# Self-attention on one core: compact reciprocals by DMA, even score slots, weighted values two key chunks at a time, and three short chains of probability tiles

## The chip, the core and the metric

The kernel runs on one core of a Trainium2 chip. Five engines work side by side and meet only through semaphores: TensorE (PE in the profile, its weight loads PEld), VectorE (DVE), ScalarE (ACT), GpSimd (POOL) and SyncE (SP, which here only issues DMAs). The metric is the device time of one execution in microseconds. Before the change it is 3310.52 us, the median of three runs (3309.83 to 3311.77).

## The reference

A decoder layer over x of shape (2, 2048, 512): layer norm and self-attention, cross-attention to 154 context rows, and a feed-forward part with a shared and eight chosen experts. The change touches the self-attention alone. Cut to it:

```python
B, S, D = (2, 2048, 512); H = 16; HEAD_DIM = 32; BLOCK = 512
qkv = (layernorm(x) @ w_qkv.T)                     # q, k, v: (b, H, s, 32)
for k_blk, v_blk in blocks_of(k, v, BLOCK):        # a softmax that is built up block by block
    scores = einsum('bhid,bhjd->bhij', q, k_blk) / sqrt(32)
    ...
    out = ... + exp(block_max - new_lse) * einsum('bhij,bhjd->bhid', exp(scores - block_max), v_blk)
x = x + out @ w_out.T
```

That equals softmax(q k^T / sqrt(32)) v for each head. The kernel works it out in two passes: the row maxima first, then the exponentials, their sums and the weighted values.

## The kernel before, in words

`self_attention` runs over 32 **units**. A unit is one batch, four heads (a quad) and a block of 512 queries; four units in a row share a quad's keys and values. A unit has 16 **steps** `k`, one for each chunk of 128 keys. In step `k` PE does, in this order (`body` of the tensor block):

- for each of the four heads, the transposed scores of the **next** chunk (`transposed_scores`, L698, into `ps_st`, three banks), and between them some **score slots** of the **next unit** (`scores`, L679, into `ps_s`, three banks). A slot is 128 queries by 512 keys of one head, and only its row maximum is wanted. A unit has 64 slots; `SLOTS_AT` says how many stand in each step, and 8 early ones stand in steps 14 and 15 of the unit before that.
- in steps 7 and 14 (`TURN_AT`) four small matmuls (`turn_max`, L690) that turn half of the next unit's row maxima into a row, which ACT copies into `q_stack` (L861, L862). Before step 15 PE waits until ACT has copied the second half, because the next unit's transposed scores start there.
- the weighted values of chunk `k` (`weighted_values`, L709, four heads side by side in four column strips, accumulated in `ps_pv`), a group of four fp32 matmuls that the trace shows as eight. After step 8 and step 14 a group of the same shape follows that sums a tile of probabilities over the keys with `ones` (L717, `TOTALS_AT`), and after step 3 one for the unit before (`added_totals`, L724). These sums are the softmax denominators, in `ps_d`.

ACT takes each transposed score tile from its bank with an exponential (L880) into `probs`, a ring of 8 chunks, and at a unit's end copies `ps_pv` to `attn_raw` (L886). DVE takes each score slot with a maximum (L778, `slot_max`); a bank of `ps_s` is free for PE again only when its maximum is done (`max_done`). POOL adds up ten of the 16 probability chunks in `added` (`add`, L637); the other six are added in two chains of three by DMAs that accumulate in SBUF (`link`, L645, issued by POOL).

When the denominators of a unit are complete, DVE inverts `ps_d` in four pieces of 128x128 between score slots (`invert`, L803), multiplies with `attn_raw` (`normalize`, L810), and SP stores the result (L583). SP also loads queries four units ahead (L565) and, at the end of each quad, the keys and values of the quad after the next (L572, L577), on the same queue as the store.

## Time and profile before

| what | value |
|---|---|
| median of three runs | 3310.52 us |
| the profiled execution | 3310.81 us, span of its instructions 3309.0 us, mean clock 0.940 |
| self-attention in it | first score matmul at 344.2 us, last normalization at 2149.0 us |
| busy over the span | PE 3018.6 us (91%), DVE 2198.7 (66%), POOL 1725.8 (52%), ACT 1623.4 (49%) |
| DVE reciprocals of the denominators | 128 of 128x128, 121.0 us in all |
| accumulating DMAs | 128 of 1024 KB, median 7.0 us from issue to landing |

The profile's times are those of one execution and count from its first instruction. "Busy" for PE is modelled from pipelined matmuls, so 91% says that PE is nearly always holding work, not that it computes at its peak; how fast it goes is read from the starts of neighbouring matmuls. A bracket at a row's end gives the engine's idle time just before it and what ended it.

### The profile page before, as it was taken

The numbers are of one execution on the slowest core, as the hardware profiler recorded it, in microseconds if no ns is written. First come the engines' busy times: TensorE is split into PE (matmuls) and PEld (weight loads), VectorE is DVE, ScalarE is ACT, GpSimd is POOL, SyncE is SP. The second block draws the span as 40 slices with busy tenths as digits, with TensorE's granted clock in tenths as the row PEclk, the third lists the DMA queues.
The fourth block names the chain that finished last, engine by engine and source line by source line (L and its number), as shares of the span: only waits on it lengthen the run. The fifth ranks groups of instructions, "written<-read, shape, count | busy, mean of one in ns | idle before, by whom it ended". The sixth has DMA issues, their size and how long they took to land. (4 is left out here: it accounts for less than half of the span.)

```text
span 3309.0 us, 41856 instructions
## 1 busy us (share of the span) xinstructions
PE 3018.6 (91%) x15214; PEld 1726.3 (52%) x15214; DVE 2198.7 (66%) x3919; ACT 1623.4 (49%) x2965; POOL 1725.8 (52%) x697
## 2 busy tenths in 40 slices
PE   8998799999999999999999999789579995889488
PEld 5787344444444444444444444268454553777433
DVE  4331888888888888888888888255348694666323
ACT  2222166666666666666666667522136572222111
POOL 0000288888787878787878788800112001333255
PEclk9999599999999999999999999889878797999689
DMA  7444744744646446446374444269655243333621
GB/s 232 179 167 154 178 102 87 156 91 104 143 104 142 102 99 144 105 106 137 87 156 86 106 120 98 62 196 251 153 141 155 79 120 112 127 142 113 210 79 36
DMA packets 171933, 426.85 MB, mean 129 GB/s; under 512 B 19393, under 2 KB 40802, under 8 KB 151716
## 3 DMA queue, kind: packets, MB, share of 16 engines
q1 hardware_dynamic: 147614, 279.59, 28.9%
q0 software_dynamic: 24128, 144.75, 20.8%
q8 instruction: 115, 1.88, 0.2%
q14 instruction: 76, 0.62, 0.1%
HBM read 172.29 MB, written 126.67 MB: 90 GB/s over the span
## 5 line engine op out<-in xcount | busy, mean ns | idle before, releaser
L778 DVE TENSOR_REDUCE part_max<-ps_s 128x1 f32<-128x512 f32 x2048 | 1270.9, 680 | 305.4 <-PE ps_s L679 305.4
L880 ACT ACTIVATE probs<-ps_st 128x512 f32<-128x512 f32 x2048 | 1086.2, 600 | 548.3 <-PE ps_st L698 526.6
L637 POOL TENSOR_TENSOR added<-added,probs 128x2048 f32<-128x2048 f32 x256 | 1185.6, 4631 | 90.4 <-ACT probs L880 63.5
L679 PE MATMUL ps_s<-k_stack,q_stack 96*128 96x512 f32 x2048 | 841.4, 427 | 28.1 <-POOL max_parts L627 20.7
L698 PE MATMUL ps_st<-q_stack,k_stack 98*128 98x512 f32 x2048 | 861.2, 426 | 5.2 <-ACT probs L880 3.9
L698 PEld LDWEIGHTS ps_st<-q_stack,k_stack 98*128 98x128 f32 x2048 | 388.3, 190 | 508.9 <-ACT probs L880 358.8
L709 PE MATMUL ps_pv<-probs,v_sb 128*32 128x512 f32 x4096 | 549.3, 608 | 0.0
L679 PEld LDWEIGHTS ps_s<-k_stack,q_stack 96*128 96x128 f32 x2048 | 395.0, 193 | 214.5 <-DVE part_max L778 143.8
L645 POOL DMA_DIRECT2D probs<-probs x128 | 111.5, 871 | 230.3 <-PE ps_pv L709 219.2
L1366 PE MATMUL xps_s<-xks_stack,xq_stack 99*128 99x154 f32 (+1 forms) x512 | 122.8, 319 | 55.7 <-DVE xident_r L1479 48.8
L637 POOL TENSOR_TENSOR added<-probs 128x2048 f32<-128x2048 f32 x32 | 146.4, 4575 | 47.2 <-ACT probs L880 47.2
L709 PEld LDWEIGHTS ps_pv<-probs,v_sb 128*32 128x32 f32 x4096 | 80.9, 108 | 152.0 <-ACT probs L880 123.7
L1447 DVE TENSOR_REDUCE xneg_max<-xps_s 128x2 f32<-128x308 f32 x256 | 114.8, 476 | 68.1 <-PE xps_s L1369 45.9
L803 DVE RECIPROCAL ps_d<-ps_d 128x128 f32<-128x128 f32 x128 | 121.0, 950 | 57.6 <-PE ps_d L724 57.6
L1366 PEld LDWEIGHTS xps_s<-xks_stack,xq_stack 99*128 99x128 f32 (+1 forms) x512 | 114.2, 224 | 73.3 <-issue 54.0
L286 DVE TENSOR_TENSOR qk_l_out<-ps_g,qk_h_out 128x512 fp32r<-128x512 f32 x64 | 43.3, 689 | 124.9 <-ACT qk_h_out L350 124.9
L238 POOL TENSOR_TENSOR rstd<-var_eps,minus_half 128x4 f32<-128x4 f32 x8 | 8.1, 1014 | 224.2 <-DVE var_eps L264 224.2
L1393 PE MATMUL xps_st<-xq_stack,xkt_stack 98*77 98x512 f32 x256 | 118.6, 468 | 4.4 <-ACT xprobs L1511 2.4
L1511 ACT ACTIVATE xprobs<-xps_st,xpad_bias 77x512 f32<-77x512 f32 x192 | 119.1, 677 | 4.4 <-PE xps_st L1393 3.8
L1465 DVE RECIPROCAL xsums<-xsums 128x256 f32<-128x256 f32 x64 | 111.1, 1742 | 6.1 <-ACT xsums L1524 6.1
L1702 POOL MEMSET e_bias_rows<- 128x1024 f32 x1 | 1.0, 957 | 209.0 <-POOLq L46 209.0
L350 ACT ACTIVATE qk_h_out<-ps_g 128x512 fp32r<-128x512 f32 x64 | 38.3, 598 | 144.4 <-PE ps_g L398 144.4
(266 smaller groups left out, 3567.0 us busy)
## 6 DMA issues: line engine op xcount, KB each, us to landing
probs<-probs POOLq DMA_DIRECT2D x128, 1024.0 KB, 7.0
xq_stack<-q_parts SPq DMA_DIRECT2D x64, 384.0 KB, 4.5
q_stack<-q_hi SPq DMA_DIRECT2D x64, 256.0 KB, 6.3
k_stack<-k_hi SPq DMA_DIRECT2D x64, 256.0 KB, 8.7
q_parts<-q_h_out SPq DMA_DIRECT2D x64, 256.0 KB, 4.9
x_in<-in_x_rows SPq DMA_DIRECT2D x8, 1024.0 KB, 7.0
q_hi<-qk_h_out SPq DMA_DIRECT2D x8, 1024.0 KB, 4.3
q_lo<-qk_l_out SPq DMA_DIRECT2D x8, 1024.0 KB, 6.3
```

The lines of the kernel that those rows point to most:

```text
L637: pool.tensor_tensor(added[:, w % 2], left, probs[:, k % RING], ALU.add).then_inc(added_up, 1)
L645: pool.dma_start(probs[:, k % RING].rearrange("p j q -> p (j q)"), probs[:, (k - 1) % RING].rearrange("p j q -> p (j q)"), accum_op=ALU.ad ...
L679: pe.matmul(ps_s[:, place % BANKS], q_stack[0:ROWS, w % 4, j, t * P:(t + 1) * P], k_stack[0:ROWS, w // BPB, j, n * BLK:(n + 1) * BLK], sta ...
L698: pe.matmul(ps_st[:, n % BANKS], k_stack[0:TOP, w // BPB, j, k * P:(k + 1) * P], q_stack[:, w % 4, j], start=True, stop=True).then_inc(ite ...
L709: mm = pe.matmul(ps_pv[j * HD:(j + 1) * HD], v_sb[:, w // BPB, k, j * HD:(j + 1) * HD], probs[:, k % RING, j], start=(k == 0), stop=(k == ...
L778: dve.tensor_reduce(part_max[:, s:s + 1], ps_s[:, (w * SLOTS + s) % BANKS], AX.X, ALU.max)\
L803: dve.reciprocal(ps_d[:, cols], ps_d[:, cols]).then_inc(inverted, 1)
L880: act.activation(probs[:, k % RING, j], ps_st[:, n % BANKS], ACT.Exp, scale=SCALE).then_inc(item_used, 1)
L1366: mm = pe.matmul(out, q_stack[0:top, u % BUFS, j, t * P:(t + 1) * P], ks_stack[0:top, batch(u), u % QUADS * HEADS + j], start=True, stop=n ...
L1393: mm = pe.matmul(out, kt_stack[:, batch(u), u % QUADS * HEADS + j, h * KH:(h + 1) * KH], q_stack[0:TOP, u % BUFS, j], start=True, stop=not ...
L1447: dve.tensor_reduce(neg_max[:, u % 2, s // 2, s % 2 * 2:s % 2 * 2 + 2], ps_s[:, (u * SLOTS + s) % BANKS, 0:2 * SC].rearrange("p (t k) -> p ...
L1511: act.activation(probs[:, u % 2, t % 2, t // 2], ps_st[0:KH, n % BANKS], ACT.Exp, scale=SCALE, **bias)\
```

## The change

Five edits, all in the self-attention:

1. PE does nothing of the weighted values in even steps; in each odd step it does those of chunks `k-1` and `k` one after the other.
2. `SLOTS_AT` becomes four slots in each of steps 0 to 13 (before: 4, 4, 4, 4, 3, 3, 2, 4, 5, 5, 5, 5, 4, 4), so that with the early ones each of the 16 steps has four.
3. The two chains of three chunks become three chains of two (2+3, 6+7, 8+9), each one accumulating DMA. Their sums come after steps 9, 13 and 15, which makes three groups with `ones` in place of two. POOL issues three such DMAs per unit in place of four, and its nine adds take chunks 0, 1, 4, 5 and 10 to 15.
4. The denominators no longer are inverted in `ps_d` by DVE. ACT copies them to SBUF in step 4 (`dens_out`); SP moves one row per head to DRAM and back as 128x16; DVE inverts that in one instruction before the first slot of step 7; SP moves it to DRAM, and four DMAs read it back with each row repeated over 32 partitions into `attn_out`.
5. POOL multiplies `attn_out` with `attn_raw` (`product`) after its fifth add. The last unit alone is inverted and multiplied by DVE as before, in one piece of 128x512.

```diff
-    SLOTS_AT = [4, 4, 4, 4, 3, 3, 2, 4, 5, 5, 5, 5, 4, 4, 0, 0]
+    SLOTS_AT = [4] * 14 + [0, 0]
-    ADDED = [0, 4, 5, 9, 10, 11, 12, 13, 14, 15]
-    CHAINS = [(1, 2, 3), (6, 7, 8)]
-    TOTALS_AT = {8: 0, 14: 1}
+    ADDED = [0, 1, 4, 5, 10, 11, 12, 13, 14, 15]
+    CHAINS = [(2, 3), (6, 7), (8, 9)]
+    TOTALS_AT = {9: 0, 13: 1, 15: 2}
     LATE = 3
+    INVERT_AT = 7
+    PRODUCT_AFTER = 4
...
                 def store(i, w):
-                    sp.wait_ge(normalized, at(i, w, 1, 1))
                     unit = i * UPB + w
+                    if ends(i, w):
+                        sp.wait_ge(last_normalized, 1)
+                    else:
+                        sp.wait_ge(dens_copied, unit + 1)
+                        sp.dma_start(dens_rows, dens_sb[0:P:HD]).then_inc(dens_moved, 16)
+                        sp.wait_ge(dens_moved, 16 * (unit + 1))
+                        sp.dma_start(dens_c[:], dens_rows.rearrange("j (c e) -> (j c) e", e=HEADS * BLK // P))\
+                          .then_inc(dens_laid, 16)
+                        sp.wait_ge(inverted, unit + 1)
+                        sp.dma_start(recip_rows.rearrange("j (c e) -> (j c) e", e=HEADS * BLK // P), recip_c[:])\
+                          .then_inc(recip_moved, 16)
...
+                        sp.wait_ge(recip_moved, 16 * (unit + 1))
+                        for j in range(HEADS):
+                            sp.dma_start(attn_out[j * HD:(j + 1) * HD, w % 2], recip_rows[j].partition_broadcast(HD))\
+                              .then_inc(recip_loaded, 16)
+                        sp.wait_ge(normalized, unit + 1)
...
+                def product(i, w):
+
+                    unit = i * UPB + w
+                    pool.wait_ge(raw_done, unit + 1)
+                    pool.wait_ge(recip_loaded, 16 * HEADS * (unit + 1))
+                    pool.tensor_tensor(attn_out[:, w % 2], attn_out[:, w % 2], attn_raw[:, w % 2], ALU.mult).then_inc(normalized, 1)
...
-                        link(i, w, 0, 0)
                         add(i, w, 0)
+                        link(i, w, 0)
                         add(i, w, 1)
-                        link(i, w, 0, 1)
-                        link(i, w, 1, 0)
                         add(i, w, 2)
+                        link(i, w, 1)
                         add(i, w, 3)
-                        link(i, w, 1, 1)
+                        link(i, w, 2)
                         for n in range(4, ADDS):
                             add(i, w, n)
+                            if n == PRODUCT_AFTER and not begins(i, w):
+                                product(*unit_before(i, w))
...
-                            weighted_values(i, w, k)
+                            if k % 2:
+                                weighted_values(i, w, k - 1)
+                                weighted_values(i, w, k)
...
+                def invert(i, w):
+                    unit = i * UPB + w
+                    dve.wait_ge(dens_laid, 16 * (unit + 1))
+                    dve.reciprocal(recip_c[:], dens_c[:]).then_inc(inverted, 1)
...
+                                if not begins(i, w) and s == SLOTS_OF[INVERT_AT][0]:
+                                    invert(*ended)
                                 slot_max(*one, s)
...
+                def dens_out(i, w):
+                    unit = i * UPB + w
+                    act.wait_ge(dens_done, unit + 1)
...
+                    act.activation(dens_sb[:], ps_d[:], ACT.Copy).then_inc(dens_copied, 1)
...
+                            if k == LATE + 1 and not begins(i, w):
+                                dens_out(*unit_before(i, w))
```

PE, the end of step 14 and the start of step 15, before (L698 transposed scores, L679 score slot, L690 the turned maxima, L709 weighted values, L717 a chain's sum):

```order
L698 MATMUL ps_st<-q_stack,k_stack 128x512
L679 MATMUL ps_s<-k_stack,q_stack 128x512
L690 MATMUL ps_st<-ident_r,max_parts 64x128 x4
L709 MATMUL ps_pv<-probs,v_sb 32x512 x4
L717 MATMUL ps_d<-probs,ones 32x512 x4
L698 MATMUL ps_st<-q_stack,k_stack 128x512
L679 MATMUL ps_s<-k_stack,q_stack 128x512
```

The same place after the change (L733 transposed scores, L714 score slot, L725 the turned maxima, L744 weighted values, L752 a chain's sum):

```order
L714 MATMUL ps_s<-k_stack,q_stack 128x512
L725 MATMUL ps_st<-ident_r,max_parts 64x128 x4
L733 MATMUL ps_st<-q_stack,k_stack 128x512
L714 MATMUL ps_s<-k_stack,q_stack 128x512
L733 MATMUL ps_st<-q_stack,k_stack 128x512
L714 MATMUL ps_s<-k_stack,q_stack 128x512
L733 MATMUL ps_st<-q_stack,k_stack 128x512
L714 MATMUL ps_s<-k_stack,q_stack 128x512
L733 MATMUL ps_st<-q_stack,k_stack 128x512
L714 MATMUL ps_s<-k_stack,q_stack 128x512
L744 MATMUL ps_pv<-probs,v_sb 32x512 x8
L752 MATMUL ps_d<-probs,ones 32x512 x4
```

Before, two groups stand between the turned maxima and the next unit's first transposed scores; now none does, and three groups stand after step 15.

DVE, slots 0 to 28 of a unit, before (L778 a slot's maximum, L803 a quarter of the reciprocal, L810 the normalization):

```order
L798 TENSOR_REDUCE max_parts<-max_rest 128x2x4
L778 TENSOR_REDUCE part_max<-ps_s 128x1 x25
L803 RECIPROCAL ps_d<-ps_d 128x128
L778 TENSOR_REDUCE part_max<-ps_s 128x1
L803 RECIPROCAL ps_d<-ps_d 128x128
L778 TENSOR_REDUCE part_max<-ps_s 128x1
L803 RECIPROCAL ps_d<-ps_d 128x128
L778 TENSOR_REDUCE part_max<-ps_s 128x1
L803 RECIPROCAL ps_d<-ps_d 128x128
L778 TENSOR_REDUCE part_max<-ps_s 128x1
L810 TENSOR_TENSOR attn_out<-ps_d,attn_raw 128x512
```

After the change, from the middle of a unit on, slots 32 to 63 (L815 a slot's maximum, L840 the small reciprocal, L829 and L835 the first and last of five small reductions that close a half of the maxima):

```order
L829 TENSOR_REDUCE max_parts<-part_max 128x2x4
L830 TENSOR_REDUCE max_pair<-part_max 128x8
L831 TENSOR_REDUCE max_pair<-part_max 128x8
L833 TENSOR_REDUCE max_rest<-max_pair 128x8
L835 TENSOR_REDUCE max_parts<-max_rest 128x2x4
L815 TENSOR_REDUCE part_max<-ps_s 128x1 x4
L840 RECIPROCAL recip_c<-dens_c 128x16
L815 TENSOR_REDUCE part_max<-ps_s 128x1 x28
```

Four reciprocals and the product have left DVE's row of maxima, and one reciprocal of 16 columns, which waits for two DMAs, stands in front of the first slot of step 7.

## Rows read from the trace of the kernel before

**Rows 1.** Windows: length, PE, PEld, DVE, ACT, POOL busy, granted clock, DMA share, GB/s.
```profile
500.00:2000.00 1500.00, 1487.32 (x7947) 729.08 (x7940) 1229.80 (x2178) 1016.21 (x1906) 1227.89 (x359) 1.00 0.53 116
```

**Rows 2.** The page's costliest groups: DVE's maxima, POOL's adds, DVE's reciprocals.
```profile
L778 DVE TENSOR_REDUCE part_max<-ps_s 128x1 f32<-128x512 f32 x2048 | 1270.9, 680 | 305.4 <-PE ps_s L679 305.4
...
L637 POOL TENSOR_TENSOR added<-added,probs 128x2048 f32<-128x2048 f32 x256 | 1185.6, 4631 | 90.4 <-ACT probs L880 63.5
...
L803 DVE RECIPROCAL ps_d<-ps_d 128x128 f32<-128x128 f32 x128 | 121.0, 950 | 57.6 <-PE ps_d L724 57.6
```

**Rows 3.** Timeline, ACT alone: the copy that ends a unit, three in a row.
```profile
993.59 0.60 ACT L886 ACTIVATE attn_raw<-ps_pv 128x512 f32<-128x512 f32 x1 [0.59 <-PE ps_pv L709]
...
1047.72 0.60 ACT L886 ACTIVATE attn_raw<-ps_pv 128x512 f32<-128x512 f32 x1 [0.59 <-PE ps_pv L709]
...
1102.83 0.60 ACT L886 ACTIVATE attn_raw<-ps_pv 128x512 f32<-128x512 f32 x1 [0.57 <-PE ps_pv L709]
```

**Rows 4.** Timeline, PE alone: a step with four slots that ends in two groups.
```profile
1002.60 0.50 PE L698 MATMUL ps_st<-q_stack,k_stack 98*128 98x512 f32 x1
...
1004.34 0.39 PE L679 MATMUL ps_s<-k_stack,q_stack 96*128 96x512 f32 x1
1004.66 1.07 PE L709 MATMUL ps_pv<-probs,v_sb 128*32 128x512 f32 x8
1005.54 1.04 PE L724 MATMUL ps_d<-added,ones 128*32 128x512 f32 x8
1006.51 0.50 PE L698 MATMUL ps_st<-q_stack,k_stack 98*128 98x512 f32 x1
1006.85 0.40 PE L679 MATMUL ps_s<-k_stack,q_stack 96*128 96x512 f32 x1
```

**Rows 5.** Timeline: PE and DVE in a step with five slots.
```profile
1030.91 0.64 PE L679 MATMUL ps_s<-k_stack,q_stack 96*128 96x512 f32 x2
...
1031.35 3.08 DVE L778 TENSOR_REDUCE part_max<-ps_s 128x1 f32<-128x512 f32 x5 [0.46 <-PE ps_s L679]
...
1032.10 0.50 PE L679 MATMUL ps_s<-k_stack,q_stack 96*128 96x512 f32 x1
...
1032.70 0.51 PE L679 MATMUL ps_s<-k_stack,q_stack 96*128 96x512 f32 x1
...
1033.13 1.07 PE L709 MATMUL ps_pv<-probs,v_sb 128*32 128x512 f32 x8
...
1034.13 0.50 PE L698 MATMUL ps_st<-q_stack,k_stack 98*128 98x512 f32 x1
```

**Rows 6.** Timeline: the turned maxima after step 14 and ACT's copies of them.
```profile
1042.26 0.40 PE L690 MATMUL ps_st<-ident_r,max_parts 128*64 128x128 f32 x4
...
1042.98 0.58 ACT L861 ACTIVATE q_stack<-ps_st 2x512 fp32r<-2x512 f32 x1
...
1043.58 0.59 ACT L862 ACTIVATE q_stack<-ps_st 2x512 fp32r<-2x512 f32 x1
...
1044.44 0.50 PE L698 MATMUL ps_st<-q_stack,k_stack 98*128 98x512 f32 x1
```

**Rows 7.** The page's DMA issues: the store of a unit, size and median landing.
```profile
attn_t<-attn_out SPq DMA_DIRECT2D x32, 256.0 KB, 2.4
```

**Rows 8.** Timeline, SP alone: the load of a quad's values.
```profile
1050.23 0.42 SPq L577 DMA_DIRECT2D v_sb<-v_rows  x1
```

**Rows 9.** DMA issues of 1040 to 1051 us: that load's time to landing.
```profile
v_sb<-v_rows SPq DMA_DIRECT2D x1, 1024.0 KB, 21.9
```

**Rows 10.** DMA issues of 1066 to 1076 us: the store behind it.
```profile
attn_t<-attn_out SPq DMA_DIRECT2D x1, 256.0 KB, 4.4
```

**Rows 11.** Timeline, PE alone: two waits of the last unit.
```profile
2109.86 1.93 PE L717 MATMUL ps_d<-probs,ones 128*32 128x512 f32 x8 [2.52 <-DMA probs<-probs]
...
2130.33 1.07 PE L709 MATMUL ps_pv<-probs,v_sb 128*32 128x512 f32 x8
...
2143.45 1.93 PE L724 MATMUL ps_d<-added,ones 128*32 128x512 f32 x8 [7.63 <-POOL added L637]
```

More of the change, by code:

```diff
@@ L483, in self_attention @@
         attn_raw = sb("attn_raw", [P, 2, BLK])
+        dens_sb = sb("dens_sb", [P, BLK])
+        dens_c = sb("dens_c", [P, HEADS * BLK // P])
+        recip_c = sb("recip_c", [P, HEADS * BLK // P])
         attn_out = sb("attn_out", [P, 2, BLK])
@@ L497, in self_attention @@
         pv_done, dens_done, added_up = sem("pv_done"), sem("dens_done"), sem("added_up")
-        chain_summed = [sem(f"chain_summed{c}") for c in range(2)]
+        chain_summed = [sem(f"chain_summed{c}") for c in range(len(CHAINS))]
         raw_done, inverted, normalized = sem("raw_done"), sem("inverted"), sem("normalized")
+        dens_copied, dens_moved, dens_laid, recip_moved, recip_loaded = (
+            sem(n) for n in ("dens_copied", "dens_moved", "dens_laid", "recip_moved", "recip_loaded"))
+        last_inverted, last_normalized = sem("last_inverted"), sem("last_normalized")
         out_stored = [sem(f"out_stored{s}") for s in range(2)]
@@ L550, in self_attention, with ends @@
         SLOTS_OF = list(slots_of())
-        FREED = SLOTS_OF[LATE + 1][1]
+        def ends(i, w):
+            return isinstance(i, int) and i == TURNS - 1 and w == UPB - 1
         q_units = [s.rearrange("b (g j r) (n k) -> b g n r j k", g=QUADS, j=HEADS, n=BPB) for s in (q_hi, q_lo)]
@@ L827, in body @@
                             max_rows(*one, 1)
+                        else:
+                            invert(*ended)
                         if exists(*two):
@@ L836, in body @@
                     if last:
-                        for n in (UPB - 2, UPB - 1):
-                            for q in range(TPB):
-                                invert(i, n, q)
-                            normalize(i, n)
+                        normalize_last(i, UPB - 1)
                 dve.wait_ge(ident_loaded, 16)
@@ L871, in exponentials @@
                             if old % KT in chain[:-1]:
-                                links = chain.index(old % KT) + 1
-                                act.wait_ge(chain_summed[c], at(i, w, 32, 16 * links - (0 if old >= 0 else 32)))
+                                act.wait_ge(chain_summed[c], at(i, w, 16, 16 if old >= 0 else 0))
                             if old % KT == chain[-1]:
```

37 lines of the change are left out of this document (17 added, 20 removed).

## The prediction

> **What bounds the kernel now.** I read the busy times first, then the rows that mark the units, then PE's own timeline inside a unit, since the change touches nothing else. Over 1500 us of the self-attention PE is busy 1487 us at full granted clock, the four other engines have idle time [rows 1], and the ends of three units lie 54.13 and 55.11 us apart [rows 3]. The second interval is the first unit of a quad. So nearly everything is set by how closely PE's matmuls follow each other, and the question is what separates their starts.
>
> Take a step with four slots. From its first transposed score at 1002.60 to its last slot at 1004.34 there are eight matmuls; then the weighted values start 0.32 us later, the second group 0.88 us after that, the next transposed score 0.97 us after that, and its slot 0.34 us later [rows 4]. A group that stands alone goes over into the next step after 1.00 us (1033.13 to 1034.13) [rows 5]. From these I take four numbers. Neighbouring score matmuls start (1.74 - 0.34) / 6 = 0.235 us apart. A lone group adds 0.32 + 1.00 + 0.34 - 2 x 0.235 = 1.19 us. A group behind another adds 0.88 + 0.97 - 1.00 = 0.85 us. So each merge of two lone groups saves 0.34 us.
>
> The second limit is DVE with its three banks. In the step with five slots the first maximum starts 0.44 us after its slot (1030.91, 1031.35), five of them take 3.08 us, that is 0.60 us each, and the fourth and the fifth slot start only at 1032.10 and 1032.70, also 0.60 apart [rows 5]. 1032.10 is the end of the first maximum (1031.35 + 0.69) plus 0.06. So a slot cannot start before the start of the maximum three slots back plus 0.74 us. And after a slot that waited, the weighted values follow 0.43 us later, not 0.32.
>
> **The change, part by part.** *Merged weighted values and the extra group.* Eight merges per unit save 8 x 0.34 = 2.7 us; one group with `ones` more costs 0.85 us. That is -1.9 us per unit, if nothing waits.
>
> *What the bursts do to DVE's banks.* PE now offers eight slots in a row, 0.47 us apart, and DVE takes them at 0.60 us. I count from the first transposed score of a pair of steps. Slot n could start at 0.34 + 0.47n; its maximum starts at 0.78 + 0.60n; the bank allows 1.52 + 0.60(n - 3). Slots 0 to 5 pass. Slot 6 could start at 3.16 but may at 3.32; slot 7 at 3.63, but may at 3.92. The pair's first group then starts 0.43 us later and the next pair 0.88 + 0.97 us after that: 3.92 + 0.43 + 1.85 = 6.20 us. Without the wait it would be 3.63 + 0.32 + 1.85 = 5.80 us. Two single steps of four slots take today 2 x (3.91 - 0.85) = 6.12 us [rows 4]. So the merge gives almost nothing where a step already had four slots: the pause that let DVE catch up came once per four slots and now comes once per eight. What the even slots give back is that today's steps with five slots (3.55 us, 1030.58 to 1034.13) go. DVE's bursts end at 0.78 + 4.2 + 0.7 = 5.7 us, before the next pair's first slot, so the small reductions after steps 5 and 13 are hidden there.
>
> *The turned maxima after step 14.* Today two groups stand between them and the next unit's scores. ACT's two copies start 0.72 us after the turned maxima and end 1.91 us after (1042.26; 1043.58 + 0.59), and PE goes on at 2.18 us [rows 6]: hidden. In the changed order nothing stands there, so PE must wait. The fourth slot starts at 1.75, the turned maxima at 2.00, PE goes on at 2.00 + 1.91 + 0.06 = 3.97 instead of about 2.43. In return DVE has caught up, so the last four slots do not wait: the eighth starts at 3.97 + 0.34 + 3 x 0.47 = 5.72, and the pair with its three groups lasts 5.72 + 0.32 + 1.85 + 0.85 = 8.7 us. That is 1.65 us more than the 7.05 us of another pair with three groups.
>
> *ACT's copy of the denominators* (0.6 us like [rows 3]) stands between exponentials in step 4. It takes about 0.6 us of a burst in which ACT otherwise idles a little; I put it at 0.2 us of PE time, between 0 and 0.6. *DVE's small reciprocal* stands in the middle of a burst, so its time reaches PE in full: between nothing and the 0.95 us of 128 columns [rows 2], and with 16 columns near the low end, 0.2 us. The 3.8 us of old reciprocals per unit come off DVE where PE hardly waited. *POOL* has 9 adds of 4.6 us [rows 2], three issues and a product, some 45 us of 55: it keeps its slack, as today (1228 of 1500 us busy) [rows 1].
>
> Sum for a unit, by pairs of steps: 6.20; 7.05 (added sums); 6.40 (copy); 6.65 (reciprocal 0.2, turned maxima 0.25); 7.05; 6.20; 7.05; 8.70. Together 55.3 us against 54.13: **+1.15 us**.
>
> *The four DMA hops.* The copy is ready 3.2 us into the third pair. Two hops at the 2.4 us of a store on the same queue [rows 7], with 0.1 us each for the handover, bring the denominators back at 8.2 us. DVE asks for them at 6.4 + 3.1 = 9.5 us. So 1.3 us of margin, and the way back has a whole unit. In the first unit of a quad it is different: the values load, asked for at 1050.23, lands 21.9 us later [rows 8, 9], 24.4 us after the unit's end mark at 1047.72 [rows 3], and a store issued behind it on the queue takes 4.4 us [rows 10], landing as the load ends. The changed unit asks for its loads some 1.4 us earlier, so the first hop lands at about +23.5 us and the second at +26; DVE asks at 6.2 + 7.05 + 9.5 - 0.2 = 22.6. Less competition from the accumulating DMAs may take 2 us off. I take a wait of 2.5 us, between 0 and 4. Such units come six times: 55.3 + 2.5 - 55.11 = **+2.7 us** each.
>
> *The last unit* ends with POOL: PE waits 7.63 us for its last add [rows 11]. POOL issues one DMA less, waits for no chain of two, and starts with less in arrears; I take 5 us off, at most 7.6.
>
> Total: 25 units x 1.15 = 29, 6 x 2.7 = 16, less 5: +40 us. Made against the profiled execution's 3310.8 us, which stands 0.3 above the median: **3350 us**.
>
> **The rivals.** *Late hops in every unit, 0.13.* The first hop leaves while an accumulating DMA of 1 MB is still moving. If both hops took 4.4 us as in [rows 10], the denominators would be back at 3.2 + 9.0 = 12.2 us, 2.7 us late also in the 25 units where I have no wait: 67 us more, 3417 us. For it speaks that the overlap is certain; against it that the 4.4 us are explained by a load on the same queue. It decides from a hop of about 3 us on. The Trainium skill bears on this (DMA: Bandwidth & Descriptors, Queues, rings and completion order): a DMA engine empties a whole packet of several descriptors from one ring before it turns to the next, so a small transfer can sit behind much of a large one. No row of mine shows a small hop under such a load.
>
> *The clock falls in the new waits, 0.07.* In the last unit PE idles 2.52 us and comes back with a group that takes 1.93 us, not 1.04, at half clock, and is back at 1.07 us only by 2130.33, 20 us later [rows 11]. If the wait of 2.5 us in six units did that, some 10 us each are lost: 3410 us. Against it: PE is busy all around, while in the last unit it has no slots. The Trainium skill (TensorE: Matmul & The Clock Gate, HAM oscillation) says that idle gaps between bursts bring the throttle back again and again; by that the repeated waits are the danger.
>
> *Same time, 0.08.* If the copies after step 14 were hidden after all (ACT's part of 1.5 us gone), the 31 units give back 47 us: 3303 us. Nothing in the order hides them.
>
> *Faster, 0.12.* If the bursts did not wait for banks, pairs would take 5.80 and 6.65 us, a unit 55.3 - 7 x 0.40 = 52.5 us, and the whole 40 - 87 = -47: 3264 us. It decides on one thing, whether DVE starts a maximum every 0.60 us or faster than 0.52. The rows show 0.60 at every place where DVE is behind.
>
> **How the numbers follow.** My forecast, bank waits plus the wait after step 14 plus the quads' wait, has 0.60, and it alone reaches from 3322 (no wait in the quads, no cost of copy and reciprocal) to 3375. To hold 8 in 10 the range takes in part of the late hops: 3322 to 3400 us. What a measurement of this kernel can tell from no change is 0.2%, 6.6 us. Slower 0.80 (0.60 + 0.13 + 0.07), same 0.08, faster 0.12.
>
> **What would show it.** In the changed trace: slots 6 and 7 of a burst 0.60 us apart and weighted values 0.43 us behind; ordinary units of 55.3 us; PE idle for 1.5 us before the first transposed score of step 15, released by ACT's second copy; DVE idle before the small reciprocal only in the first unit of a quad, about 2.5 us, released by a DMA. I am wrong if units are below 54.1 us, if DVE waits for the DMA in every unit, or if the granted clock of 500 to 2000 us is no longer 1.00.

## The result, and the profile after

The changed kernel takes 3354.0 us, the median of 4 runs (3345.05 to 3362.33); the kernel before took 3310.18 us in the same comparison (4 runs, 3308.95 to 3311.77). The ratio is 1.0132, with a 95% interval of 1.0105 to 1.0159: slower by 1.3%. The forecast was 3350 us in a range of 3322 to 3400. The profiled execution took 3352.46 us, its span 3350.7 us.

The windows view of the changed kernel, which answers to [rows 1]. Its columns are: stretch, its length, busy time (and instructions) of PE, PEld, DVE, ACT and POOL, granted clock, DMA share, GB/s. The last line is a short stretch to which I come back.

```profile
500.00:2000.00 1500.00, 1457.62 (x7992) 734.54 (x7992) 1096.76 (x2025) 967.06 (x1890) 1214.66 (x352) 0.99 0.46 100
...
836.80:840.20 3.40, 3.40 (x17) 0.79 (x20) 1.31 (x3) 0.73 (x2) 3.40 (x1) 0.50 0.91 236
```

PE was busy 1487 us of the 1500 before and is busy 1458 now, and DVE has lost 133 us of work (above all its large reciprocals and the multiplications). So PE waits more, though DVE has less to do.

The costliest groups of the changed kernel's page, against [rows 2]: DVE's maxima and POOL's adds.

```profile
L815 DVE TENSOR_REDUCE part_max<-ps_s 128x1 f32<-128x512 f32 x2048 | 1252.0, 682 | 461.4 <-PE ps_s L714 461.4
...
L666 POOL TENSOR_TENSOR added<-added,probs 128x2048 f32<-128x2048 f32 x256 | 1198.9, 4683 | 130.5 <-ACT probs L914 111.7
```

A maximum costs what it cost, but DVE's idle time ahead of the maxima rose from 305 to 461 us: its reciprocals are gone, and it gets its slots in bursts with long pauses between. POOL is no nearer to being the bound (111.7 us of waiting for `probs`, before 63.5).

ACT's timeline, the copy that ends a unit, three in a row, against [rows 3]. The last column is idle time and what ended it.

```profile
729.69 0.60 ACT L920 ACTIVATE attn_raw<-ps_pv 128x512 f32<-128x512 f32 x1 [2.28 <-PE ps_d L752]
...
784.76 0.60 ACT L920 ACTIVATE attn_raw<-ps_pv 128x512 f32<-128x512 f32 x1 [2.29 <-PE ps_d L752]
...
841.47 0.60 ACT L920 ACTIVATE attn_raw<-ps_pv 128x512 f32<-128x512 f32 x1 [3.94 <-PE ps_d L752]
```

A unit takes 55.07 us, 0.94 more than the 54.13 of before, and one like that which ends at 841.47 takes 56.71. Units that begin a quad used to take more than the others (55.11 us in [rows 3]); now they are ordinary, all but one.

**Inside a unit.** PE's timeline in the first pair of steps of a unit, to be laid beside [rows 4, 5]: the first transposed score, slots 5 to 7, the two groups, and the next pair's first transposed score.

```profile
784.56 0.50 PE L733 MATMUL ps_st<-q_stack,k_stack 98*128 98x512 f32 x1
...
787.27 0.50 PE L714 MATMUL ps_s<-k_stack,q_stack 96*128 96x512 f32 x1
...
787.87 0.50 PE L714 MATMUL ps_s<-k_stack,q_stack 96*128 96x512 f32 x1
...
788.47 0.50 PE L714 MATMUL ps_s<-k_stack,q_stack 96*128 96x512 f32 x1
788.90 1.92 PE L744 MATMUL ps_pv<-probs,v_sb 128*32 128x512 f32 x16
790.76 0.50 PE L733 MATMUL ps_st<-q_stack,k_stack 98*128 98x512 f32 x1
```

Slots 6 and 7 start 3.31 and 3.91 us into the pair (predicted 3.32 and 3.92) and 0.60 apart, which is DVE's pace; the early ones stand 0.47 apart. The weighted values follow 0.43 us behind the last slot, and the next pair begins at 6.20. By pairs, an ordinary unit of the changed kernel measures 6.20, 7.06, 6.23, 6.53, 7.06, 6.20, 7.06 and 8.72 us from first transposed score to first transposed score; predicted were 6.20, 7.05, 6.40, 6.65, 7.05, 6.20, 7.05 and 8.70.

The timeline behind step 14, PE and ACT, against [rows 6].

```profile
777.81 0.40 PE L725 MATMUL ps_st<-ident_r,max_parts 128*64 128x128 f32 x4
...
778.55 0.58 ACT L896 ACTIVATE q_stack<-ps_st 2x512 fp32r<-2x512 f32 x1
...
779.15 0.59 ACT L897 ACTIVATE q_stack<-ps_st 2x512 fp32r<-2x512 f32 x1
...
779.78 0.50 PE L733 MATMUL ps_st<-q_stack,k_stack 98*128 98x512 f32 x1 [1.57 <-ACT q_stack L897]
```

The chain of copies that was covered is now bare: PE idles 1.57 us, released by ACT's second copy, in every unit that has a next one.

**The clock.** The same place one unit later, PE alone.

```profile
834.85 0.50 PE L733 MATMUL ps_st<-q_stack,k_stack 98*128 98x512 f32 x1 [1.57 <-ACT q_stack L897]
...
836.96 3.51 PE L744 MATMUL ps_pv<-probs,v_sb 128*32 128x512 f32 x16
840.30 1.03 PE L752 MATMUL ps_d<-probs,ones 128*32 128x512 f32 x8
841.26 0.50 PE L733 MATMUL ps_st<-q_stack,k_stack 98*128 98x512 f32 x1
```

Sixteen matmuls that took 1.92 us at 788.90 take 3.51 us here, and the windows line 836.80 to 840.20 above gives the granted clock as 0.50, that is 1.2 GHz, with PE busy for the whole of it. It had idled for 1.57 us and worked again for 2 us before it fell. This happens in 8 of the 31 units and costs 1.64 us each time (56.71 - 55.07). The Trainium skill (TensorE: Matmul & The Clock Gate, HAM oscillation) warns of idle gaps that come back again and again; in its example they are DMA waits of some 3 to 5 us, and the clock falls at every one. This trace agrees in part: its gap of 1.57 us is shorter, comes back in every unit, and has a fall behind it in 8 of them.

**The denominators.** DVE's timeline around its small reciprocal, and below it SP's issues of the hops of that unit and of the next, which begins a quad.

```profile
640.45 0.25 DVE L840 RECIPROCAL recip_c<-dens_c 128x16 f32<-128x16 f32 x1 [0.64 <-DMA dens_c<-dens_rows]
...
804.83 2.49 DVE L815 TENSOR_REDUCE part_max<-ps_s 128x1 f32<-128x512 f32 x4 [0.54 <-PE ps_s L714]
807.23 0.24 DVE L840 RECIPROCAL recip_c<-dens_c 128x16 f32<-128x16 f32 x1
```

```profile
801.02 0.49 SPq L597 DMA_DIRECT2D dens_rows<-dens_sb  x1
804.32 0.34 SPq L599 DMA_DIRECT2D dens_c<-dens_rows  x1
807.50 0.34 SPq L602 DMA_DIRECT2D recip_rows<-recip_c  x1
808.98 1.72 SPq L608 DMA_DIRECT2D attn_out<-recip_rows  x4
...
857.72 0.50 SPq L597 DMA_DIRECT2D dens_rows<-dens_sb  x1
861.95 0.34 SPq L599 DMA_DIRECT2D dens_c<-dens_rows  x1
864.20 0.33 SPq L602 DMA_DIRECT2D recip_rows<-recip_c  x1
```

SP issues a hop when the one before has landed. The first hop takes 3.3 us from issue to the next issue (4.2 in the unit that begins a quad), the second at most 2.9 until DVE uses it (2.0), the third, on its way back, 1.5. DVE finds the denominators there at 807.23, and in the quad's first unit at 863.93 too. Only once in the units with slots, at 640.45, does it wait, 0.64 us; that is the first unit of the quad before. There the first hop had taken 5.1 us, and the second shows its own length: 1.8 us from its issue at 638.65 to the reciprocal.

What holds the first hop is the accumulating DMA that POOL has issued 3.7 us before it, at 797.36 and at 854.06. The DMA view's issues of 797 to 797.9 and of 854 to 854.9 us give its size and its time to landing:

```profile
probs<-probs POOLq DMA_DIRECT2D x1, 1024.0 KB, 6.9
...
probs<-probs POOLq DMA_DIRECT2D x1, 1024.0 KB, 7.9
```

797.36 + 6.9 is 804.3 and 854.06 + 7.9 is 862.0: SP goes on to the second hop (804.32, 861.95) when that DMA lands. The two agree within 0.1 us in 25 of the 31 units. So 8 KB sit out nearly the whole of a transfer of 1 MB that left before them; this is the small hop under a load for which the prediction had no row. The load of the quad's values, asked for at 841.41, is not what holds it: from 856.9 to the hop's issue at 857.72 only the accumulating DMA moves.

**The end of the stage.** ACT's marks of the last two units, against 2026.87, 2080.78 and 2135.94 before, and DVE's last normalization, at 2149.0 before.

```profile
2061.12 0.60 ACT L920 ACTIVATE attn_raw<-ps_pv 128x512 f32<-128x512 f32 x1 [2.31 <-PE ps_d L752]
...
2121.89 0.60 ACT L920 ACTIVATE attn_raw<-ps_pv 128x512 f32<-128x512 f32 x1 [3.38 <-PE ps_d L752]
...
2169.78 0.60 ACT L920 ACTIVATE attn_raw<-ps_pv 128x512 f32<-128x512 f32 x1 [2.10 <-PE ps_d L752]
```

The next to last unit took 60.8 us, where it had taken 53.9. ACT's and PE's timelines say why:

```profile
2077.18 1.94 ACT L946 ACTIVATE k_stack<-k_stack 128x2048 fp32r<-128x2048 f32 x1
```

```profile
2079.67 0.80 PE L733 MATMUL ps_st<-q_stack,k_stack 98*128 98x512 f32 x1 [1.68 <-ACT probs L914]
...
2080.82 3.64 PE L744 MATMUL ps_pv<-probs,v_sb 128*32 128x512 f32 x16
```

ACT has a large copy here that prepares the next stage's weights. It stands in the middle of a merged burst, PE fills its banks of transposed scores, waits 1.68 us, and the clock is at half from 2079.3 to 2086.1 on top. The same unit then has a second fall, from 2116.8 to 2120.2, like those of the others.

**The account.** The stage ended at 2149.7 us before and ends at 2187.4 now, +37.7: units 1 to 29 at +0.94 are 27.3, eight falls of the clock 13.1, the one late hop 0.7, the units that begin a quad give back 6.7 and small delays of other units of before 0.6, the next to last unit is +6.9, the last one with its end -3.4, and the stage starts 0.5 later; that is 37.8. The stages behind it took 4 us more (1163.3 against 1159.4 us) in these two executions, and the span grew by 41.7.

### The profile page after: what moved, and what is told of

Same layout as the page of the kernel before. It is cut to its first block and busy times, and to the rows that moved or that the text cites. A ratio compares the mean times of both kernels' runs of the same rounds, so it can differ in the third digit from the quotient of the medians.

```text
span 3350.7 us, 42483 instructions
## 1 busy us (share of the span) xinstructions
PE 3023.3 (90%) x15470; PEld 1752.2 (52%) x15470; DVE 2073.0 (62%) x3792; ACT 1593.5 (48%) x2996; POOL 1733.9 (52%) x696
## 3 DMA queue, kind: packets, MB, share of 16 engines
q0 software_dynamic: 19520, 111.19, 15.6%
q8 instruction: 117, 1.92, 0.2%
## 5 line engine op out<-in xcount | busy, mean ns | idle before, releaser
L815 DVE TENSOR_REDUCE part_max<-ps_s 128x1 f32<-128x512 f32 x2048 | 1252.0, 682 | 461.4 <-PE ps_s L714 461.4
L914 ACT ACTIVATE probs<-ps_st 128x512 f32<-128x512 f32 x2048 | 1046.1, 619 | 541.5 <-PE ps_st L733 541.3
L666 POOL TENSOR_TENSOR added<-added,probs 128x2048 f32<-128x2048 f32 x256 | 1198.9, 4683 | 130.5 <-ACT probs L914 111.7
L714 PE MATMUL ps_s<-k_stack,q_stack 96*128 96x512 f32 x2048 | 896.0, 444 | 21.5 <-POOL max_parts L656 20.7
L733 PE MATMUL ps_st<-q_stack,k_stack 98*128 98x512 f32 x2048 | 849.2, 417 | 55.0 <-ACT q_stack L897 49.8
L733 PEld LDWEIGHTS ps_st<-q_stack,k_stack 98*128 98x128 f32 x2048 | 387.8, 190 | 347.5 <-issue 186.5
L714 PEld LDWEIGHTS ps_s<-k_stack,q_stack 96*128 96x128 f32 x2048 | 394.0, 192 | 298.6 <-DVE part_max L815 236.5
L744 PE MATMUL ps_pv<-probs,v_sb 128*32 128x512 f32 x4096 | 508.3, 615 | 0.0
L744 PEld LDWEIGHTS ps_pv<-probs,v_sb 128*32 128x32 f32 x4096 | 108.7, 111 | 225.6 <-ACT probs L914 123.5
L672 POOL DMA_DIRECT2D probs<-probs x96 | 83.7, 872 | 213.8 <-PE ps_pv L744 208.9
L1083 POOL TENSOR_TENSOR c_rstd<-c_var_eps,c_minus_half 128x4 f32<-128x4 f32 x8 | 8.1, 1010 | 183.5 <-DVE c_var_eps L1113 183.5
```

The costliest lines, as they stand in the source:

```text
L666: pool.tensor_tensor(added[:, w % 2], left, probs[:, k % RING], ALU.add).then_inc(added_up, 1)
L672: pool.dma_start(probs[:, k % RING].rearrange("p j q -> p (j q)"), probs[:, (k - 1) % RING].rearrange("p j q -> p (j q)"), accum_op=ALU.ad ...
L714: pe.matmul(ps_s[:, place % BANKS], q_stack[0:ROWS, w % 4, j, t * P:(t + 1) * P], k_stack[0:ROWS, w // BPB, j, n * BLK:(n + 1) * BLK], sta ...
L733: pe.matmul(ps_st[:, n % BANKS], k_stack[0:TOP, w // BPB, j, k * P:(k + 1) * P], q_stack[:, w % 4, j], start=True, stop=True).then_inc(ite ...
L744: mm = pe.matmul(ps_pv[j * HD:(j + 1) * HD], v_sb[:, w // BPB, k, j * HD:(j + 1) * HD], probs[:, k % RING, j], start=(k == 0), stop=(k == ...
L815: dve.tensor_reduce(part_max[:, s:s + 1], ps_s[:, (w * SLOTS + s) % BANKS], AX.X, ALU.max)\
```

## The experiments

All ratios are to the kernel before, run beside each kernel on the same chip; the chip is not the same for all of them, so ratios and not times are to be compared. "Unit" is the distance between unit marks that recur in ordinary units, or its range where falls of the clock change it; 55.07 us in the changed kernel, 54.13 before.

| run | median us (range, runs) | ratio, 95% | unit us |
|---|---|---|---|
| each step | 3293.6 (3272.5 to 3299.9, 10) | 0.9936 [0.9915, 0.9957] | 53.62 |
| sum after 14 | 3305.9 (3287.8 to 3309.5, 10) | 0.9971 [0.9951, 0.9991] | 53.57 |
| both | 3262.0 (3255.9 to 3284.1, 4) | 0.9867 [0.9814, 0.9919] | 53.00 |
| short maxima | 3294.4 (3280.1 to 3301.3, 10) | 0.9952 [0.9925, 0.9979] | 52.53 or 54.16 |
| even alone | 3373.0 (3364.2 to 3381.2, 4) | 1.0183 [1.0156, 1.0209] | 55.3 to 57.7 |
| merge alone | 3433.1 (3422.6 to 3454.5, 4) | 1.0376 [1.033, 1.0421] | 57.2 to 60.7 |
| both, inverted later | 3267.2 (3265.7 to 3273.5, 4) | 0.9880 [0.9838, 0.9921] | 53.0 |
| both, two chains | 3274.0 (3253.8 to 3281.8, 4) | 0.9875 [0.9824, 0.9926] | 52.3 |
| two chains, inverted later | 3282.1 (3269.8 to 3285.5, 5) | 0.9904 [0.9867, 0.9942] | 52.3 |
| late split | 3331.4 (one run) | none | 55.06 |

**Each step: the changed kernel with the weighted values of one chunk per step.**

```diff
-                            if k % 2:
-                                weighted_values(i, w, k - 1)
-                                weighted_values(i, w, k)
+                            weighted_values(i, w, k)
```

> The changed kernel with one line undone: the weighted values of each chunk in their own step again. Bank theory (the pause for DVE must come once per four slots; a burst of eight slots waits 0.40 us per pair): 16 steps of 3.06 us, four more groups of 0.85, turned maxima 0.5, and after step 14 a wait that one group hides only in part (0.64 us): 53.5 us per unit against 55.07, and no fall of the clock: about 3292 us. Rival (a lone group costs 0.34 us more than a merged one and that is all there is to it): 8 x 0.34 = 2.7 us per unit more, less 1 us after step 14: about 3405 us.

Measured: 53.62 us a unit, 3293.6 us in all. Steps of four slots take 3.06 us, or 3.92 with a sum; two of them make 6.12, against the 6.20 of a merged pair. So the merge in this order is worth less than nothing. The wait after step 14 shrinks from 1.57 to 0.56 us, since one group of weighted values now stands in it, and between 500 and 2000 us the clock falls once, where it fell eight times. That one fall (1496.8) doesn't follow a wait of 0.56 us but another: DVE had waited 2.04 us for the denominators of a quad's first unit, and PE 1.29 us for DVE. In all six first units DVE now waits 1.1 to 2.0 us. In the profiled executions the stage ends 57.2 us sooner: 29 units by 1.44 are 41.8, seven falls fewer 11.5, the next to last unit 6.0, the last 1.8, the earlier start 1.7, less 5.3 that the quads' first units cost more; together 57.5. The whole is 60.4 us shorter.

**Sum after 14: the pairs stay, but steps 14 and 15 are single, and the third chain's sum comes after step 14, between the turned maxima and the next scores.**

```diff
-    TOTALS_AT = {9: 0, 13: 1, 15: 2}
+    TOTALS_AT = {9: 0, 13: 1, 14: 2}
...
-                            if k % 2:
+                            if k >= KT - 2:
+                                weighted_values(i, w, k)
+                            elif k % 2:
```

> The changed kernel with the weighted values of step 14 done in step 14, and the third chain's sum after them instead of after step 15; all other pairs merged. Theory of the uncovered copy: the last two steps take 4.18 + 3.06 = 7.24 us instead of 8.72, and without the idle PE the falls of the clock (eight of 1.64 us) are gone: about 3295 us. Rival (the wait before step 15 is not on the path, the bursts alone make the unit long): within 5 us of 3352, falls as before.

Measured: 53.57 us in ordinary units, as expected: pairs of 6.20, 7.06, 6.23, 6.54, 7.05, 6.20, 7.05, then steps of 4.16 and 3.08. The 1.50 us a unit are all in the last two steps, where the wait after step 14 is gone. But the whole came to 3305.9, some 11 us above the expectation, because the units that begin a quad now took 55.3 to 58.0 us. DVE's and PE's timelines in one of them:

```profile
849.46 0.25 DVE L842 RECIPROCAL recip_c<-dens_c 128x16 f32<-128x16 f32 x1 [1.67 <-DMA dens_c<-dens_rows]
```

```profile
850.31 0.50 PE L714 MATMUL ps_s<-k_stack,q_stack 96*128 96x512 f32 x1 [1.74 <-DVE part_max L817]
...
850.98 3.10 PE L744 MATMUL ps_pv<-probs,v_sb 128*32 128x512 f32 x16
```

That is the wait for the denominators that I had forecast for the changed kernel, though not by way of the load: DVE stops 1.67 us for the DMA, PE 1.74 us for DVE, and the group behind it runs at half clock (3.10 us for 1.92). It comes in all six such units (1.7 to 2.8 us), and behind four of them the clock falls. A faster unit asks earlier, and the accumulating DMA in front of the hop, issued at 837.84, took 11.4 us to land; the margin is used up.

**Both: single groups in every step and the sum after step 14.** The edit is the two above together (`weighted_values(i, w, k)` in every step, `TOTALS_AT = {9: 0, 13: 1, 14: 2}`).

> Both edits together: weighted values in each step, third chain's sum after step 14. Bank theory and copy theory add up: 53.5 - 0.64 = 52.9 us per unit, about 3272 us, faster than the kernel before. Rival (merging saves): slower than the run with step 14 alone by 7 x 0.34 = 2.4 us per unit, about 3370 us.

Measured: 53.00 us, 3262.0 us, 1.3% faster than before. PE's timeline behind step 14:

```profile
764.11 0.40 PE L725 MATMUL ps_st<-ident_r,max_parts 128*64 128x128 f32 x4
764.44 1.06 PE L744 MATMUL ps_pv<-probs,v_sb 128*32 128x512 f32 x8
765.32 1.04 PE L752 MATMUL ps_d<-probs,ones 128*32 128x512 f32 x8
766.29 0.50 PE L733 MATMUL ps_st<-q_stack,k_stack 98*128 98x512 f32 x1
```

The next scores follow 2.18 us after the turned maxima with no wait, the very distance that [rows 6] show before. The clock doesn't fall between 500 and 2000 us. So all that the changed kernel loses per unit sits in two choices: the pairing and the place of the third sum.

The size of the gain needs care. The windows view of the stages behind the self-attention:

```profile
2114.00:3257.80 1143.80, 938.39 (x4654) 621.72 (x4654) 634.94 (x1166) 358.45 (x619) 267.09 (x261) 0.88 0.46 139
```

Of the 51.2 us by which this profiled execution is shorter than that of the kernel before, 35.7 lie in front of the end of the self-attention (2114.0 against 2149.7), and 15.5 behind it (1143.8 against 1159.4), in stages that the edits don't touch. That expectation and measurement lie within 10 us of each other is in part luck.

**Short maxima: DVE made faster.** The kernel is the changed one, with maxima over 384 of the 512 columns of each slot, so part of the row maxima is left out; the scale is made small so that the exponentials stay finite.

```diff
-    SCALE = float(HD) ** -0.5
+    SCALE = 0.05 * float(HD) ** -0.5
...
-                    dve.tensor_reduce(part_max[:, s:s + 1], ps_s[:, (w * SLOTS + s) % BANKS], AX.X, ALU.max)\
+                    dve.tensor_reduce(part_max[:, s:s + 1], ps_s[:, (w * SLOTS + s) % BANKS, 0:BLK - P], AX.X, ALU.max)\
```

> The changed kernel, but DVE takes the maximum of the first 384 of the 512 columns of each score slot (part of the row maxima is left out, and the softmax scale is 0.05 times the right one so that exponentials stay finite; PE's and ACT's work is unchanged in size). Bank theory: a maximum every 0.47 us instead of 0.60, no slot waits, pairs of 5.80 and 6.65 us instead of 6.20 and 7.06: 52.3 us per unit, about 3265 us, with the 1.5 us wait after step 14 still there. Rival (PE is slow in the bursts for another reason): units of 55 us.

PE's and DVE's timelines of a first pair of steps:

```profile
764.35 0.50 PE L733 MATMUL ps_st<-q_stack,k_stack 98*128 98x512 f32 x1
...
768.00 0.40 PE L714 MATMUL ps_s<-k_stack,q_stack 96*128 96x512 f32 x1
768.33 1.92 PE L744 MATMUL ps_pv<-probs,v_sb 128*32 128x512 f32 x16
770.18 0.50 PE L733 MATMUL ps_st<-q_stack,k_stack 98*128 98x512 f32 x1
```

```profile
765.12 3.87 DVE L815 TENSOR_REDUCE part_max<-ps_s 128x1 f32<-128x384 f32 x8 [4.01 <-PE ps_s L714]
```

Eight maxima take 3.87 us instead of 4.88, DVE now keeps up with PE, which gives it a slot each 0.47 us (its own pace with 384 columns isn't seen here), the last slot starts 3.65 us into the pair (predicted 3.63) and the pair takes 5.83, where my working without bank waits gave 5.80. That isolates the bank waits: 0.4 us a pair, as reckoned. The unit falls to 52.53 us where the clock holds, but it holds in few: 24 of the 31 units have a fall, and the median one takes 54.16 us (granted clock 0.97 over the 1500 us). So the whole missed its expected 3265 by 29 us, and by a cause that I had not put in.

**Even alone: the kernel before with four slots in every step.**

```diff
-    SLOTS_AT = [4, 4, 4, 4, 3, 3, 2, 4, 5, 5, 5, 5, 4, 4, 0, 0]
+    SLOTS_AT = [4] * 14 + [0, 0]
```

> The kernel before with the even score slots alone (four in each of steps 0 to 13). Bank theory: the steps with five slots (3.55 us) become steps of 3.06, the four large reciprocals in steps 4 to 6 now stand between four slots a step instead of three and cost 1 to 2 us there: 53.6 us per unit, about 3294 us. Rival (the gain of evenness is eaten whole by the reciprocals, which is why the old table was uneven): 54.1 us or more, 3310 us or more.

Measured: 1.8% slower. I had expected a gain. DVE's timeline says what the old table was for:

```profile
743.18 0.96 DVE L803 RECIPROCAL ps_d<-ps_d 128x128 f32<-128x128 f32 x1
744.04 0.63 DVE L778 TENSOR_REDUCE part_max<-ps_s 128x1 f32<-128x512 f32 x1
```

Each reciprocal sets a maximum back by 0.86 us, and PE waits for it, so step 5 takes 5.5 us and step 6 3.8, and a unit 55.3. The clock adds to it: in 17 of the 31 units it falls, though no single wait of PE is longer than 0.7 us, and those units take 56.1 us and more. The thin steps (3, 3, 2) had made room for the four reciprocals. So even slots are not a gain of their own. No run has the small reciprocal with the old slots; what evenness adds to it isn't shown.

**Merge alone: the kernel before with the pairs.**

```diff
-    TOTALS_AT = {8: 0, 14: 1}
+    TOTALS_AT = {8: 0, 13: 1}
...
-                            weighted_values(i, w, k)
+                            if k % 2:
+                                weighted_values(i, w, k - 1)
+                                weighted_values(i, w, k)
```

> The kernel before with the merged weighted values alone (old slots, old chains, the second chain's sum after step 13 because chunk 14 is now done in step 15). Bank theory: pairs with ten slots take 7.4 us, the pair with the reciprocals about 7.8, the last pair 7.85 because nothing covers ACT's copies: 56.7 us per unit and falls of the clock: about 3400 us. Rival (merging saves 0.34 us eight times per unit): 3310 - 84 = 3226 us.

Measured: 3.8% slower, 57.2 to 57.9 us a unit without a fall of the clock and up to 60.7 with. A pair with ten slots takes 7.39 us. The working that gave 6.20 for eight slots gives 6.20 + 2 x 0.60 = 7.40 for ten: each slot past the sixth costs DVE's 0.60, not PE's 0.47. That is the second check of the bank rule, at another size.

**Both, inverted later: DVE asks for the denominators two steps later.**

```diff
-    INVERT_AT = 7
+    INVERT_AT = 9
```

> The run with weighted values in each step and the third sum after step 14, with the small reciprocal before the first slot of step 9 instead of step 7. Theory of the late hops in the first unit of a quad (DVE waits there for the denominators behind the load of the values): the six first units of 54.2 to 55.1 us become 53.0, 9 us less in all: about 3253 us. Rival (these units are longer for another reason, the loads themselves slow PE or ACT): unchanged, 3262 us.

The windows line of this kernel:

```profile
500.00:2000.00 1500.00, 1500.00 (x8374) 772.54 (x8372) 1166.35 (x2120) 1028.72 (x1981) 1273.83 (x369) 1.00 0.47 103
```

PE is busy for all of the 1500 us. The units that begin a quad fell from 54.2 to 55.1 to the 53.0 of all others, and the stage ended 9.3 us sooner than in the run before it (2104.7 against 2114.0). The whole time doesn't show it: the ratios are 0.9880 and 0.9867, with intervals that overlap. In the profiled executions the stages behind took 1160.7 us here and 1143.8 there. That the 9 us would show in enough runs is likely and not shown.

**Both, two chains: the old two chains of three tiles, with one sum fewer.** The diff is cut to the tables; the second issue of a chain and the waits for it come back with them.

```diff
-    ADDED = [0, 1, 4, 5, 10, 11, 12, 13, 14, 15]
-    CHAINS = [(2, 3), (6, 7), (8, 9)]
-    TOTALS_AT = {9: 0, 13: 1, 14: 2}
+    ADDED = [0, 4, 5, 9, 10, 11, 12, 13, 14, 15]
+    CHAINS = [(1, 2, 3), (6, 7, 8)]
+    TOTALS_AT = {8: 0, 14: 1}
```

> Weighted values in each step, even slots and reciprocals by DMA as in the changed kernel, but the two chains of three chunks of the kernel before (sums after steps 8 and 14). Theory (a group of four fp32 matmuls behind another costs 0.85 us and nothing hides it): 52.98 - 0.85 = 52.13 us per unit, less up to 7 us in all that the second accumulating DMA may cost in quads' first units: 3236 to 3243 us. Rival (the sum after step 9 fills a pause that DVE needs anyway, so that dropping it gives nothing): 3262 us.

Measured: 52.15 us at best, so the group with `ones` is worth 0.85 us, as priced. But the median unit is 52.3, and those that begin a quad take 54.4 to 58.8. DVE's timeline in one:

```profile
842.99 0.25 DVE L841 RECIPROCAL recip_c<-dens_c 128x16 f32<-128x16 f32 x1 [3.08 <-DMA dens_c<-dens_rows]
```

Whole: 3274.0 where I expected 3236 to 3243, and by the ratio no better than the three chains. In the profiled execution the stage ends 4.2 us sooner than with three (2109.8; 2.1 of it is an earlier start), but the stages behind take 1170.2 us, the longest of all.

**Two chains, inverted later.** The edit is `INVERT_AT = 9` in the kernel above.

> Both edits: the old two chains and the small reciprocal before step 9. If both theories hold, they add: 3227 to 3234 us, with all units near 52.1 us. If the quads' first units are held by the accumulating DMA instead, they stay about 1 us longer and the time is about 3236.

Measured: 3282.1, where I expected 3227 to 3234. The best units stay at 52.13; those that begin a quad still take 54.2 to 59.5, now with the wait at step 8, where the sum of the first chain stands. PE's timeline in one of them:

```profile
637.51 1.93 PE L755 MATMUL ps_d<-probs,ones 128*32 128x512 f32 x8 [2.51 <-DMA probs<-probs]
```

PE itself waits for the accumulating DMA, 1.8 to 3.8 us in all six such units, and in four of them the clock falls. DVE waits for the denominators in one only. That is the second case of the expectation, at 2 to 7 us a unit where I had put 1. So the third chain costs one group per unit and takes away a DMA that has to wait for another before the sum can come.

**Late split: does ACT's large copy do the harm of the next to last unit because it meets the denominators' copy in one step?**

```diff
-                            if last and w == UPB - 2 and k in (4, 11):
-                                n = (4, 11).index(k)
+                            if last and w == UPB - 2 and k in (6, 11):
+                                n = (6, 11).index(k)
```

> The changed kernel with ACT's first copy of the next stage's weights (1.94 us, in the last unit but one) after step 6 instead of step 4, where ACT now also copies the denominators. Theory (two extra copies in one step of ACT starve PE and the clock falls): that unit goes from 60.8 us to 56 to 58 us. Rival (the unit is long because of other loads): still above 60 us.

ACT's and PE's timelines where the copy stands now:

```profile
2083.99 1.93 ACT L946 ACTIVATE k_stack<-k_stack 128x2048 fp32r<-128x2048 f32 x1
```

```profile
2086.46 0.50 PE L733 MATMUL ps_st<-q_stack,k_stack 98*128 98x512 f32 x1 [1.21 <-ACT probs L914]
...
2087.56 3.37 PE L744 MATMUL ps_pv<-probs,v_sb 128*32 128x512 f32 x16
```

The third pair is back at 6.25 us, and the fourth takes 9.43: the stall moved with the copy. The unit takes 60.06 us against 60.77. So it isn't the meeting of the two copies; a copy of 1.9 us in a merged burst stalls PE at either of the two places tried. The whole time of this single run (3331.4) says nothing of the edit: the stage ends at 2189.4, 2 us later than in the changed kernel, and the stages behind took 1140.2 us in place of 1163.3. In the run with single groups and the later reciprocal the same unit, its copies in the old place, takes 54.1.

## Why the prediction was right, and where it was off

**The bank rule held.** "A slot cannot start before the start of the maximum three slots back plus 0.74 us" gave 6.20 and 7.05, measured 6.20 and 7.06; 5.80 without the wait, measured 5.83 with short maxima; 7.40 for ten slots, measured 7.39. The rival that the bursts don't wait (0.12) is dead.

**The wait after step 14 held**: 8.70 predicted, 8.72 measured. Filling the hole gave back 1.50 us a unit. The rival that the copies are hidden (0.08) is dead.

**The copy of the denominators was over-sized.** I put it at 0.2 us; the third pair takes 6.23, so it costs 0.03. The *reciprocal* took 0.24 us for my 0.2; the fourth pair with the turned maxima came to 6.53, not 6.65. With these the unit came out 0.94 us longer than before, not 1.15.

**The quads' wait was a wrong term, 16 us.** I had the first hop land at +23.5 us, with the load's end, and the second at +26, when DVE asks at 22.6. Measured from the unit's first transposed score at 841.26: the load was over by +15.6, before the first hop was issued at +16.5; this hop waited for the accumulating DMA alone and had landed by +20.7, and the second was there when DVE asked at 863.93, +22.7. The load took at most 15.5 us from its issue, and 21.9 before [rows 9]. I had allowed 2 us for less competition from accumulating DMAs; before, one left amid the load (1057.13), now the first leaves near its end (854.06). That this made the load shorter is likely and was not tested by itself. The step that asked the time of DVE was right, and the margin was small, so the wait appeared as soon as the unit became shorter (1.67 us in the run with the sum after step 14, 3.08 with two chains), and it went when the reciprocal stood two steps later. In the changed kernel these units even lost the 1.0 us that they cost before: falls of the clock aside, the six together came to about the time of before, where I had +16 us.

**The late hops in every unit (0.13) did not come**, although the first hop does take 3.3 us under the accumulating DMA. The rival needed both hops slow. The second mostly starts as that DMA has landed, and takes 1.8 us where it can be read; 3.3 + 1.8 is 5.1 of the 6.2 us between the first hop's issue (801.02) and the reciprocal (807.23). The margin left is 1.1 us, for my 1.3.

**The clock fell, but not where my rival put it.** I had tied it to the quads' waits and priced it at 10 us each. It fell behind the wait after step 14, which my main forecast contained, and cost 1.64 us each time, 13.1 us in all. It was absent from the forecast's sum, and by my own list of signs (a granted clock of 500 to 2000 us no longer 1.00; it is 0.99) this part of the forecast was wrong. With the 6.9 us of the next to last unit, which I had not looked at on its own, it stands in the place of the 16 us that did not come. So the total of +40 against a measured +43.8 (3354.0 - 3310.2) is partly luck: errors that cancel. And 3375, the upper end that I gave to the main forecast alone, is not the sum of its own bounds: those of the copy, the reciprocal and the quads' wait add 31 x (0.4 + 0.75) + 6 x 1.5 = 45 us to 3350, which is 3395; the stated range up to 3400 covers it.

**The last unit** gave back 3.4 us and not 5.

What each part is worth in the end: compact reciprocals with even slots, which no run takes apart, are the gain (units of 53.0 against 54.13, together with three chains, and 52.1 at best with two); the pairing costs 1.45 us a unit with its longer wait and 0.57 without it (53.57 - 53.00); the place of the third sum costs 1.50, or 0.62 if the groups are single (53.62 - 53.00). The best kernels here are those with both undone, at 0.987 to 0.990 of before; their order among themselves isn't shown.

**Open.** Which of thirty equal waits of 1.57 us is followed by a fall of the clock isn't explained: it was eight in the changed kernel, from 836.8 on every fourth, and 24 units had a fall with short maxima, whose wait is the same. The wait's length doesn't decide it: with two chains PE waited 2.39 us once without a fall, and with even slots in the old kernel the clock fell behind waits of 0.7 us. And the time of the stages behind the self-attention differs by up to 30 us between profiled executions of these kernels (1140.2 to 1170.2), which hides an effect of 9 us. Much of that is the clock as well: behind the stage PE stands at half clock for 270 us in the run with single groups and the sum after step 14, for 296 in the kernel before and 317 with two chains. Why these stretches differ isn't known.

## What to carry to other kernels

Putting two groups of the bound engine's work together saves the changes between them (0.34 us each here), but it doubles the burst that the neighbour must swallow with the same few buffers; count slot by slot against the buffers before trusting an average, and look into each burst for the neighbour's odd large instruction. Before moving work, list what its old place covered: here two groups covered a chain of copies that nobody waited for as long as they stood there. Judge the parts of a change in the company in which they are to work: even slots and merged groups each made the old kernel slower, and yet the fastest kernels here, with their small reciprocals, have even slots. And when a small transfer is on a tight schedule, look at what large transfer left just before it.

## What the runs showed of the hardware

- An idle time of PE of 1.57 us, with PE busy before and after, was followed 1.5 to 2 us later by 3.4 us at 1.2 GHz in 8 of 31 units (granted clock 0.50 from 836.80 to 840.20) and in 24 of 31 when the pairs were shorter; it cost 1.64 us each time. No fall followed the waits of 0.56 us in the run with single groups; its one fall followed a wait of 1.29 us. The kernel with PE busy throughout had none.
- In the last unit of the kernel before, PE was back at its full pace only after 20 us [rows 11]; amid steady work it was back after 3.4 us. So a price read at the end of a stage, as mine was, doesn't hold inside it.
- A hop of 8 KB, issued 3.7 us after a DMA that adds 1 MB, was done when that one landed, in 25 of 31 units within 0.1 us: 3.3 us from its issue to the next hop's, 4.2 us where the large one took 7.9 us in place of 6.9. With that DMA landed or near its end, hops took 1.8 us (the second, at 638.65) and 1.5 us (the third).
- A maximum of 128x512 from PSUM is listed with 680 ns, but a row of them runs at 0.60 us each (eight in 4.88 us). With 384 columns eight took 3.87 us, at the rate of PE's slots, 0.47 us each.
